# All six pieces of the first patch chunk in the split form, with single buffers to make room

## The reference, cut to what matters

```
tokens = einsum('bpi,hi->bph', patches, W) + b          # 2352 -> 128
h = concat([class_token, tokens]) * pos_embed
h = h + attention(layernorm(h))                          # softmax over the queries
h = h + experts(layernorm(h))                            # 32 experts, 2 per row
h = h + decay_mixing(layernorm(h))
h = h + experts(layernorm(h))                            # 16 experts, 2 per row
```

## Time and profile before

| | us |
|---|---|
| median of 3 runs | 1286.27 |
| lowest and highest | 1285.39, 1287.85 |
| the profiled execution | 1299.48 |
| its span, first to last instruction | 1297.8 |
| busy: TensorE, VectorE, GpSimd, ScalarE | 1004.7, 875.6, 703.5, 512.7 |

### The profile page before, as it was taken

The page is one execution under the profiler, slowest core; times in us unless marked ns, Lnnn a source line. Parts: engine busy times, 40 slices in busy tenths (PEclk is TensorE's granted clock), DMA queues, the critical chain, the costliest instruction groups (busy, mean ns, idle before and its releaser), DMA issues.

```text
span 1297.8 us, 22134 instructions
## 1 busy us (share of the span) xinstructions
PE 1004.7 (77%) x6263; PEld 848.0 (65%) x6263; DVE 875.6 (67%) x3298; ACT 512.7 (40%) x1345; POOL 703.5 (54%) x653
## 2 busy tenths in 40 slices
PE   6999999999999536666674666366624999999995
PEld 3566776767676525555674665256524999999995
DVE  1487888888888635455665665476643777788785
ACT  1254535544553211111332333254421555565552
POOL 1036657776775455656546566555563455555554
PEclk8998999999999657766876667576656999999998
DMA  9655566566630325557775553244244767899883
GB/s 373 268 204 178 177 239 206 206 216 221 222 126 19 108 76 164 170 161 220 241 211 172 145 154 104 73 154 159 78 139 141 248 219 245 266 323 307 289 290 131
DMA packets 121049, 247.96 MB, mean 191 GB/s; under 512 B 21787, under 2 KB 88555, under 8 KB 114656
## 3 DMA queue, kind: packets, MB, share of 16 engines
q1 hardware_dynamic: 76224, 190.74, 44.1%
q0 software_dynamic: 19584, 34.70, 8.0%
q10 hardware_dynamic: 25120, 21.12, 5.4%
HBM read 203.03 MB, written 47.46 MB: 193 GB/s over the span
## 4 chain that ended last, share of the span: by engine, by line
PE 40%; DVE 25%; issue 14%; another core or an unknown queue 8%; DMA 5%; ACT 3%; SPq 3%; ACTq 2%; DVEq 0%; POOL 0%; POOLq 0%
PE ps L882 9%; PE ps L864 6%; PE ps L685 4%; PE ps L682 3%; DMA xin<-lists_L 3%; PE ps L746 2%; PE ps L730 2%; DVE xin L1743 2%; PE ps L845 2%; DVE xin L1724 2%; SPq L532 2%; PE ps L678 2%; PE ps L703 1%; DVE ntok L1382 1%
## 5 line engine op out<-in xcount | busy, mean ns | idle before, releaser
L1969 POOL DMA_INDIRECT results_L<-xin x322 | 318.4, 989 | 278.0 <-DVE xin L1743 164.7
L1942 POOL DMA_INDIRECT lists_L<-rows,slots x250 | 280.2, 1121 | 191.8 <-issue 172.7
L685 PE MATMUL ps<-xin,w_emb 128*128 128x512 f32 x280 | 133.7, 614 | 10.0 <-DMA w_emb<-in_w_main 10.0
L882 PE MATMUL ps<-xin,QK 128*128 128x128 f32 x804 | 115.4, 294 | 29.1 <-DVE xin L1743 13.7
L882 PEld LDWEIGHTS ps<-xin,QK 128*128 128x128 f32 x804 | 106.3, 208 | 32.7 <-issue 26.3
L882 PE MATMUL ps<-xin,UH 128*128 128x128 f32 x800 | 114.0, 293 | 13.0 <-DVE xin L1743 9.6
L845 PE MATMUL ps<-ident,xin 128*128 128x128 f32 x322 | 76.0, 326 | 53.7 <-DMA xin<-lists_L 33.5
L882 PEld LDWEIGHTS ps<-xin,UH 128*128 128x128 f32 x800 | 105.9, 208 | 15.4 <-issue 14.4
L1065 ACT ACTIVATE h0T<-ps 128x256 f32<-128x256 f32 x81 | 30.8, 383 | 205.0 <-remote 75.6
L864 PE MATMUL ps<-x_hi,x_lo 128*128 128x256 f32 x320 | 99.1, 310 | 9.9 <-DVE x_lo L1718 7.5
L1951 POOL TENSOR_TENSOR x_lo<-xin,x_hi 128x2048 fp32r<-128x2048 f32 x13 | 60.1, 4625 | 76.6 <-ACT x_hi L1046 76.3
(11 more groups left out here) (275 smaller groups left out, 2420.3 us busy)
## 6 DMA issues: line engine op xcount, KB each, us to landing
xin<-in_x_main SPq DMA_DIRECT2D x48, 1536.0 KB, 7.1
xin<-in_w_L SPq DMA_DIRECT2D x80, 578.0 KB
xin<-in_w_L SPq DMA_DIRECT2D x89, 128.0 KB
xin<-lists_L SPq DMA_DIRECT2D x80, 132.0 KB
xin<-in_w_L ACTq DMA_DIRECT2D x73, 128.0 KB
xin<-in_difference SPq DMA_DIRECT2D x13, 640.0 KB
xin<-in_distance SPq DMA_DIRECT2D x13, 640.0 KB
x_hi<-results_L SPq DMA_DIRECT2D x11, 640.0 KB
```

The source lines that it names most:

```text
L685: mm = pe.matmul(psE[h], w_emb[:, k, :], xin[h][c][:, n, :], start=(k == 0), stop=False, skip_group_check=True)
L882: mm = pe.matmul(o, hTb[p2][:, f, q * 128:(q + 1) * 128], w2[:, f * D:(f + 1) * D], start=(f == 0), stop=(f == l.FC - 1))
L1942: pool.indirect_dma_start(out=lists[l.name], out_offset=bass.IndirectOffsetOnAxis(ap=slots_of(l, g, h)[:, t, k:k + 1], axis=0), in_=buf[:, ...
L1969: pool.indirect_dma_start(out=results[l.name], out_offset=bass.IndirectOffsetOnAxis(ap=xblk[u][:, q, PLACE:PLACE + 1].bitcast(U32), axis=0 ...
```

## The change

The constant `KS` goes from 4 to 6, so from group 3 on all six pieces of the first chunk are in the split form. `x_hi0`, `x_lo0` and the weights' parts grow by half. To make room, the rest of the patches, the values, the probabilities and the transposed rows are in one buffer each (`XT` keeps 640 columns, which a later stage uses). No wait is added for the last three. With a single buffer for the rest, its load for group g-1 is issued between the second and third chunk of group g, behind a wait for the last chunk of group g-2.

```diff
-FIRST, KS = 3, 4
+FIRST, KS = 3, 6
...
-        xrest = [sb(f"xrest{h}", [KREST, GP]) for h in range(2)]
+        xrest = [sb("xrest", [KREST, GP])] * 2
...
-        XT = sb("XT", [D, 2 * GT])
-        x1T = [XT[:, h * GT:(h + 1) * GT] for h in range(2)]
+        XT = sb("XT", [D, TILES * WIDE])
+        x1T = [XT[:, 0:GT]] * 2
...
-        V = [sb(f"V{h}", [SEQ, GI, D]) for h in range(2)]
+        V = [sb("V", [SEQ, GI, D])] * 2
...
-        Pr = [sb(f"Pr{h}", [SEQ, GI, SEQ]) for h in range(2)]
+        Pr = [sb("Pr", [SEQ, GI, SEQ])] * 2
...
             def load_patches(g, h, j):
                 for c in range(CHUNKS):
+                    if c == CHUNKS - 1 and g > 1:
+                        load_rest(g - 1)
                     sp.wait_ge(chunk_used[h][c], j)
...
-                    if c == CHUNKS - 1:
-                        sp.dma_start(xrest[h][:, :], a["x_rest"][bass.ds(g, 1), :, :]
-                                     .rearrange("o p n -> (o p) n")).then_inc(chunk_in[h][c], 16)
+                if g == 0:
+                    load_rest(0)
+
+            def load_rest(g):
+                h = g % 2
+                if g > 0:
+                    sp.wait_ge(chunk_used[1 - h][CHUNKS - 1], (g - 1) // 2 + 1)
+                sp.dma_start(xrest[h][:, :], a["x_rest"][bass.ds(g, 1), :, :]
+                             .rearrange("o p n -> (o p) n")).then_inc(chunk_in[h][CHUNKS - 1], 16)
             pairs(sp, load_patches)
+            load_rest(GROUPS - 1)
```

## The result

| us | before | after |
|---|---|---|
| median | 1286.27 | 1352.83 |
| lowest, highest of 5 | 1285.39, 1291.12 | 1340.63, 1356.90 |
| the profiled execution | 1299.48 | 1356.90 |
| its span | 1297.8 | 1355.2 |

The ratio is 1.0478, with a 95% interval of 1.0439 to 1.0517: the change costs 66.6 us. The code behind the change lies nine lines lower: the GpSimd subtraction is now L1960, the comparisons L1525, their sum L1530, the rank product L783, the transposes of the normalized rows L712, ScalarE's two copies L1048 and L1055.

A forecast was written before the change was run, and what follows sets the result against it. It took the front stage to be bound by TensorE and an equally long GpSimd cycle; 28.6 us of longer subtraction plus 47 us of clock falls, less 1 or 2, added 74 us to 1286.27: 1360 us, range 1318 to 1380.

The forecast's parts named there:

- TensorE's saving, counted at 0: Front, groups 3 to 15: two more split pieces save 0.34 us a step, hidden by a wait; bounds 0 and -4.4 us.
- ScalarE's copy, single buffers, late rest load, 0 each: Front steps: copy 0.84 us longer but covered, buffers without new waits, load early enough; 0 us for each.
- the wait for the normalized rows: TensorE's wait before the normalized rows' transposes, 0.17 us before the change, was to stand at 0.5 us.
- GpSimd's subtraction: Front steps: 3072 columns take 6.94 us, +2.31, of which 2.2 us a step is uncovered, 28.6 us over 13 steps.
- the stall: TensorE's idle time before the rank product, about 2.2 us in each front step, released by VectorE.
- the end of the comparisons: VectorE's two one-hot comparisons, held by the subtraction, were to end 0.4 us behind it.
- the step of 27.5: One front step, rank product to rank product, was to take 27.5 us where the clock is 1.00.
- The rival by which most of the subtraction is a fixed cost: Front: subtraction stays under 4.7 us and doesn't hold GpSimd's cycle, TensorE gains up to 4.4 us: 1282 us, chance 6%.
- The clock: Front: TensorE idling lowers its granted clock in nearly every one of 13 steps; 12 x 3.9 = 47 us, bounds 0 and 59.
- The rival by which the clock holds: Front: TensorE's granted clock stays up, so only the 28.6 us of GpSimd's longer cycle is lost: 1315 us, chance 17%.
- The sum: 28.6 + 47 = 75.6 us less 1 or 2, so 74 us added to the 1286.27 median: 1360 us.
- the ring: GpSimd's front cycle of slots, scatters and subtraction, as long as TensorE's step; 2.2 us longer a step, 28.6 us in all.

The follow-up runs named there:

- The third experiment: Changed kernel with GpSimd subtracting only four pieces, the low part of pieces 4 and 5 zero: 1175.98 against 1175.09 us for the kernel before.
- the first experiment: Changed kernel with KS back at 4, so only single buffers and the late load of the rest: 1178.73 against 1175.09 us for the kernel before.
- the second experiment: Changed kernel with TensorE multiplying pieces 4 and 5 in plain form, GpSimd still subtracting six: 1215.32 against 1175.09 us for the kernel before.
- the fourth experiment: Changed kernel with the six-piece subtraction in three back-to-back instructions of two pieces: 1224.20 against 1175.09 us for the kernel before.
- the last experiment: Changed kernel with the last two pieces' subtraction waiting for the scaled probabilities: 1191.97 against 1175.15 us for the kernel before.

## Why the prediction came out right, step by step

It said 1360 us, in a range of 1318 to 1380; measured 1352.83. The mechanism is the one forecast; that the number is so close is in part luck, as the sum shows.

**TensorE's saving, counted at 0.** Right. The third experiment has it in the work (4.1 us) and in the wait (4.6 us), and nothing of it in the time.

**ScalarE's copy, single buffers, late rest load, 0 each.** Right, by the third and the first experiment. In the profile of the changed kernel the wait for the normalized rows is 0.6 us at its longest, forecast 0.5.

**GpSimd's subtraction.** Forecast 6.94 us, measured 6.81; the stall forecast at 2.2, measured 1.86 to 2.18; the end of the comparisons 0.4 behind, measured 0.42; the step of 27.5, measured 27.48 to 27.56. Over the thirteen steps the forecast was 28.6 less 1 or 2, and the run with the stall filled measured 28.2. The rival by which most of the subtraction is a fixed cost is out: 1024, 2048, 2560 and 3072 columns took 2.4, 4.6, 5.7 and 6.8 us.

The Trainium skill ("SBUF — State Buffer", Who interferes with whom) says that a VectorE instruction with at most one input in SBUF, outside the two-port modes, does not contend with GpSimd, and that `tensor_tensor`, the comparisons' instruction, has no such mode. With this the trace with the ramp in PSUM agrees: 0.56 us against 4.65 under the same subtraction.

**The clock.** This is the mis-sized term: "12 x 3.9 = 47 us". The falls came at ten stalls of thirteen, in both profiles of the changed kernel, and filling the stalls gave back 31 to 34 us, so 3.1 to 3.4 us a fall. On the forecast's own base, the profile before with its one stall and fall of 5.3 us (337.40 - 332.07), the term measured 26 to 29. Two of its three factors were taken too high: 12 falls more than before, where it was 9, and a low stretch of 8 us, where the eleven measured (two of them in one step) were 3.4 us (five), 6.8 (five) and 10.2 (one), 6.1 us a fall. The third, 0.48 us lost for each microsecond at the low level, was about right: 31.3 us for 64.9 us in the second profile of the changed kernel is 0.48, 33.0 for 61.4 in the first 0.54 (392.86 - 359.90 = 33.0). The steps with one stretch of 3.4 us took 29.3 to 29.6 us; the longest, 34.5 us, had two stretches, 6.8 and 3.4.

The rival by which the clock holds is out; its 1315 us lay just outside the stated range, which was said to take in most of it. The Trainium skill ("TensorE: Matmul & The Clock Gate", HAM oscillation) warns of a fall behind idle gaps that are longer than any of these stalls. Here the trace disagrees: stalls of 1.9 to 2.2 us were followed by a fall in ten of thirteen steps, and with the stalls filled there was none.

**The sum.** On the forecast's own base, profile against profile, the change was to add 74 us; it added 57.4, of which 55.5 are in the thirteen steps. Those are made up of the ring (359.90 - 332.07 = 27.8) and the falls (33.0), less the stall and fall that the profile before had already (5.3). So the sum was 17 us too high, and all of that lies in the term of the clock. The medians differ by 66.6 us, 9 more than the profiles, because the profiled execution of the kernel before lay so far above its median; the forecast put its 74 us on the median, and the two errors partly cancelled. That is the luck in it. No trace of the kernel before on that chip shows an execution near the median, so how the 9 us divide between the front stage and the rest is not shown; behind the rank product of group 13 the six profiles on this kind of chip take 872 to 880 us, a spread nearly as large as the 9 us.

How many stalls are followed by a fall stays open. With the stall at about 2 us it was ten and ten on the kind of chip where the kernel before takes 1286 to 1288 us, five and six (the second and the fourth experiment) on the 1175 us kind; at 1.3 to 1.6 us three (one of them behind the 2.6 in group 12), at 1.0 to 1.1 us two of ten (the last experiment), at 0.4 to 1.1 us none but the one at 2.16. In the kernel before, the stall of 1.09 us in group 1 was followed by a fall, those of 1.06 and 1.09 in group 12 of its two profiles were not. On the one chip that ran five pieces, the ramp in PSUM and the changed kernel, the order is clear: one, three and ten falls of thirteen, each from one profile. The chance for a given stall is not. That the difference comes from the chips, and not from the edits, is only argued: the fourth experiment does on TensorE what the changed kernel does, and had six; the changed kernel itself was not run there.

Also open is the late copy of the transposed rows. It stands in both profiles of the changed kernel, twice with the ramp in PSUM, once with five pieces, and once in the profile of the kernel before, in the step of its fall; all on the 1288 us kind of chip, and never in the run in which the clock held. On the other kind it is in no run, even in steps with a fall, and there a fall cost less: (370.56 - 359.90) / 5 = 2.1 us in the second experiment. Nothing was tried on it.

## What to carry to other kernels

A kernel whose busiest engine is nine tenths busy can still have a second engine that walks a ring of the same length; before work is moved to that engine, follow the ring from instruction to instruction and find its slack, here 0.1 us. Work of GpSimd that reads SBUF costs VectorE whatever two-input instruction falls under it. Cutting it in pieces gave VectorE one instruction at a seam and not in every step, so it helps little where several are waiting; putting one of their operands in PSUM freed them, and the next instruction with two inputs in SBUF was held in their place. Price a new stall of TensorE of 2 us in the middle of dense work at its length and about as much again for the clock (here 28 and 31 to 34 us; on the other kind of chip less), and test the second half by filling the stall with products.

## What was not expected of the hardware

Three GpSimd instructions without a gap cost the pair of comparisons as much as one long one, 4.9 us for a pair that takes 0.56: in ten steps of thirteen the first comparison passed at the seam and the second was caught by the next subtraction, in three both waited for the last.

Fractions of a microsecond of stall went with much of the clock's loss: a stall shorter by 0.6 us (1.3 to 1.6 instead of 1.9 to 2.2) was worth 32.6 us over the kernel, four times its own length over thirteen steps (7.8).

The hold seems to work the other way round, too. The tenth scatter of a step, and the subtraction of the last chunk on VectorE above which it lies, in the changed kernel:

```profile
...
245.32 0.99 POOL L1951 DMA_INDIRECT lists_L<-rows,slots  x1 [0.31 <-issue]
246.62 3.67 POOL L1951 DMA_INDIRECT lists_L<-rows,slots  x1 [0.30 <-issue]
...
```

```profile
...
246.08 3.35 DVE L1356 TENSOR_TENSOR x_lo<-xin,x_hi 128x3072 fp32r<-128x3072 f32 x1
...
```

The scatter takes 3.67 us instead of 0.99, and ends at 250.29, 0.86 us behind VectorE's subtraction of two SBUF inputs (249.43). The kernel before has the same, 3.35 us, also 0.86 us behind the earlier trace rows, and the distance is 0.86 or 0.87 us in the steps of every run here. That the scatter is held, and not slow for another reason, is read from this distance alone; no run took the subtraction away.
